# A two-layer kernel with routed experts: the block list in two parts, and results stored at the addresses of their rows

## The reference

```python
x = x + mix(_layernorm(x))              # layer 0: a token-wise mixing step
# layer 0: nine experts, every token goes to two of them
logits = xf @ Wr                        # xf = _layernorm(x), 4096 x 128; Wr 128 x 9
topk_w, topk_idx = top_k(softmax(logits), 2)
gate   = silu(einsum('th,ehi->tei', xf, Wg))        # Wg, Wu 9 x 128 x 352
hidden = gate * einsum('th,ehi->tei', xf, Wu)
out    = einsum('tei,eih,te->th', hidden, Wd, cw)   # Wd 9 x 352 x 128
x = x + out
x = x + attention(_layernorm(x))        # layer 1: 16 heads, causal
x = x + moe64(_layernorm(x))            # layer 1: 64 experts, top 8, and a shared one
```

## Time and profile before

| | |
|---|---|
| median of 3 runs | 1076.92 us (1076.34 to 1079.82) |
| the profiled execution | 1076.07 us, of which the span of the trace is 1074.3 us |
| PE busy | 930.9 us (87%) |
| DVE busy | 833.0 us (78%) |
| ACT busy | 700.1 us (65%) |
| POOL busy | 455.2 us (42%) |
| chain that ended last | PE 74%, POOL 7%, DVE 6%, issue 4%, ACT 4%, DMA 3% |
| routing and scatters | 0 to 136 us of the span |
| the 72 blocks | 136.5 to 295.5 us |

### The profile page before, as it was taken

How to read it: one execution, slowest core, us unless ns; L and a number is a source line. 1 busy time by engine, 2 the same in 40 slices (tenths; PEclk the granted TensorE clock), 3 DMA queues, 4 the chain that set the end, 5 groups by cost and what they waited for, 6 DMA issues and landing times.

```text
span 1074.3 us, 20489 instructions
## 1 busy us (share of the span) xinstructions
PE 930.9 (87%) x6052; PEld 744.9 (69%) x6052; DVE 833.0 (78%) x1945; ACT 700.1 (65%) x1390; POOL 455.2 (42%) x523
## 2 busy tenths in 40 slices
PE   3652089999828999999999998999999999999998
PEld 2541079999825677776776766777777777777786
DVE  6888267777649888888888767888887979787965
ACT  4751045555436787787787766777778777777876
POOL 1278750000066565565564422444434443443433
PEclk8655589999959999999999999999999999999999
DMA  8011112222121011011010003847566575748483
GB/s 258 23 49 57 56 53 67 65 63 64 55 59 28 21 31 31 21 31 31 21 31 21 11 2 88 177 110 165 135 140 147 129 162 114 169 106 189 98 195 77
DMA packets 63921, 89.99 MB, mean 84 GB/s; under 512 B 16559, under 2 KB 54610, under 8 KB 59730
## 3 DMA queue, kind: packets, MB, share of 16 engines
q1 hardware_dynamic: 59136, 80.33, 31.2%
q0 software_dynamic: 4096, 8.40, 2.7%
q10 hardware_dynamic: 594, 0.09, 0.0%
HBM read 70.90 MB, written 17.89 MB: 83 GB/s over the span
## 4 chain that ended last, share of the span: by engine, by line
PE 74%; POOL 7%; DVE 6%; issue 4%; ACT 4%; DMA 3%; SPq 1%; POOLq 0%; DVEq 0%; ACTq 0%
POOL xs L666 6%; PE ps L2216 6%; PE ps L2198 5%; PE ps L2200 5%; PE ps L2199 5%; PE ps L2218 5%; PE ps L2217 5%; PE ps L2002 3%; PE ps L1943 3%; PE ps L2065 3%; PE ps L2048 3%; PE ps L2020 2%; PE ps L1921 2%; PE ps L1922 2%; PE ps L1923 2%
## 5 line engine op out<-in xcount | busy, mean ns | idle before, releaser
L822 POOL TENSOR_TENSOR hl<-h,hh 128x512 fp32r<-128x512 f32 x128 | 167.8, 1311 | 256.3 <-ACT hh L1100 256.3
L1100 ACT ACTIVATE hh<-h 128x512 fp32r<-128x512 f32 (+1 forms) x264 | 165.2, 626 | 33.0 <-DVE h L1778 30.2
L1778 DVE TENSOR_TENSOR h<-ps,cwB 128x512 f32<-128x512 f32 x192 | 130.1, 683 | 45.3 <-ACT ps L1089 33.8
L1678 DVE TENSOR_REDUCE nm<-ps 128x4 f32<-128x512 f32 (+1 forms) x128 | 116.4, 952 | 35.1 <-PE ps L2048 33.1
L1089 ACT ACTIVATE ps<-ps 128x512 f32<-128x512 f32 x192 | 111.6, 581 | 36.3 <-PE ps L2200 35.2
L720 POOL DMA_INDIRECT yg<-ys,gps x64 | 62.5, 976 | 166.0 <-issue 154.6
L2198 PE MATMUL ps<-xh,wh 128*128 128x512 f32 x256 | 103.7, 405 | 0.1
L2216 PE MATMUL ps<-hh,wh 128*128 128x512 f32 x256 | 102.8, 402 | 0.6 <-POOL hl L822 0.6
L1785 DVE TENSOR_TENSOR hl<-h,hh 128x512 fp32r<-128x512 f32 (+1 forms) x136 | 95.7, 703 | 9.8 <-ACT hh L1100 8.6
L2200 PE MATMUL ps<-xh,wl 128*128 128x512 f32 x256 | 100.1, 391 | 0.0
L2218 PE MATMUL ps<-hh,wl 128*128 128x512 f32 x256 | 100.0, 391 | 0.0
(11 more groups left out here) (340 smaller groups left out, 2683.2 us busy)
## 6 DMA issues: line engine op xcount, KB each, us to landing
cwB<-cwd SPq DMA_DIRECT2D x32, 1536.0 KB, 14.8
cwd<-cwS SPq DMA_DIRECT2D x64, 96.0 KB
xb<-xs SPq DMA_DIRECT2D x72, 64.0 KB, 1.8
ys<-yb SPq DMA_DIRECT2D x72, 64.0 KB, 1.6
x_res<-in_L_attn_x_dram SPq DMA_DIRECT2D x4, 512.0 KB, 6.4
wst<-in_L_ffn_W_up_dram SPq DMA_DIRECT2D x32, 64.0 KB, 2.2
wst<-in_L_ffn_W_down_dram SPq DMA_DIRECT2D x32, 64.0 KB, 2.0
out_dram<-y SPq DMA_DIRECT2D x8, 256.0 KB, 13.4
```

Of the source, the lines that this page charges most:

```text
L822: pool.tensor_tensor(hl4[:, slot(u), :], h4[:, slot(u), :], hh4[:, slot(u), :].bitcast(F32), op=ALU.subtract).then_inc(u_hlp, 1)
L1100: act.activation(hh4[r, slot(u), :], h4[r, slot(u), :], ACT.Copy).then_inc(u_hh, 1)
L1678: ins = dve.tensor_reduce(nm[:, u, 4 * g:4 * g + 4], o, axis=AX.X, op=ALU.max, negate=True)
L1778: dve.tensor_tensor(h4[:, slot(u), :], first, second, op=ALU.mult).then_inc(u_h, 1)
```

## The change

The block list is made in two parts. The first, `blk_a`, holds NFULL = 24 blocks that rounds 0 and 1 fill completely whatever the routing is. It is worked out from the counts after round 1, in small steps between the routing steps of rounds 1 to 3, and is ready behind `sel` of round 3. SP waits for it, and only for the scatters of rounds 0 and 1, and starts loading blocks, while POOL still scatters rounds 2 and 3. The whole list, `blk_b`, is worked out in single steps of 1 or 2 small DVE operations at the first ten blocks (`whole_list_step`), with nine small matmuls on PE at block 10 (`listed`), and serves blocks 24 to 71.

A block's result is now stored in `ys` at the same rows as the block has in `xs`. So `gpi` is a plain cast of the rows, but each store reads its address with a register load too. `ys` has as many rows as `xs`, rounded up to 39936, and SP fills it with zeros at the start: 13 DMAs of 3 x 1024 rows of 512 bytes, 20.4 MB in all, before them one DMA of 0.5 MB for the spare rows of `xs`. SP waits for them after it has loaded the first four blocks. The nine zero-row DMAs behind the lists' ends now stand in SP's stream after its first four steps.

The low and high parts of weight pieces 6 to 8 (Wd) are made by POOL ahead of its first scatter; DVE makes pieces 2 to 5 in step 5, and nothing of the weights is left for the first block.

```diff
+            sp_.wait_ge(consts, 1)
+            sp_.dma_start(xs[0:SPARE, :].rearrange("(k p) d -> p k d", p=P),
+                          zrow[:, :].unsqueeze(1).broadcast_to([P, SPARE // P, P])).then_inc(tails_in, 16)
+            sp_.wait_ge(consts, 2)
+            for n in range(0, NFILL, 3):
+                sp_.dma_start(ys[n * FILL * P:(n + 3) * FILL * P, :].rearrange("(n p k) d -> p n (k d)", n=3, k=FILL),
+                              zfill[:, :].unsqueeze(1).broadcast_to([P, 3, FILL * D])).then_inc(tails_in, 16)
+
+            def rows_of(blocks, b):
+                return ds(sp_.value_load(blocks[0:1, ds(b, 1)], min_val=0, max_val=SPARE + E1 * REG - P), P)
+
+            def load_block(b, u, blocks):
+                sp_.dma_start(xb[:, u, :], xs[rows_of(blocks, b), :]).then_inc(xb_in[u], 16)
...
-            def store_block(b, u):
+            def store_block(b, u, blocks):
                 sp_.wait_ge(yb_r, b + 1)
-                sp_.dma_start(ys[ds(b * P, P), :], yb[:, u, :]).then_inc(ys_out[u], 16)
+                sp_.dma_start(ys[rows_of(blocks, b), :], yb[:, u, :]).then_inc(ys_out[u], 16)
+
+            def next_block(b, u, blocks):
+                sp_.wait_ge(xT_r, b + 1)
+                load_block(b + 4, u, blocks)
+                if not isinstance(b, int) or b >= 2:
+                    store_block(b - 2, (u - 2) % 4, blocks)
+
+            sp_.wait_ge(lists, 1)
+            for s in range(2):
+                sp_.wait_ge(scat[s], SCATTERED)
+            for b in range(4):
+                load_block(b, b, blk_a)
+            sp_.wait_ge(tails_in, 16 * (NFILL // 3 + 1))
+            for b in range(4):
+                next_block(b, b, blk_a)
             sp_.wait_ge(tails, 1)
             for e in range(E1):
...
+            with sp_.Fori(1, NFULL // 4 - 1) as it:
+                for u in range(4):
+                    next_block(it * 4 + u, u, blk_a)
+            sp_.wait_ge(lists, 2)
+            sp_.wait_ge(tails_in, 16 * (NFILL // 3 + 1 + E1))
             for s in range(2):
                 sp_.wait_ge(scat[s], SCATTERED * (NR // 2))
...
+            for u in range(4):
+                next_block(NFULL - 4 + u, u, blk_b)
...
+            with sp_.Fori(NFULL // 4, NBLK // 4 - 1) as it:
                 for u in range(4):
-                    b = it * 4 + u
-                    sp_.wait_ge(xT_r, b + 1)
-                    load_block(b + 4, u)
-                    store_block(b - 2, (u - 2) % 4)
+                    next_block(it * 4 + u, u, blk_b)
             for b in range(NBLK - 6, NBLK):
-                store_block(b, b % 4)
+                store_block(b, b % 4, blk_b)
...
+            for piece in range(6, 9):
+                src, hi, lo, arrived, n = weight_piece(piece)
...
+                own.link(pool.tensor_copy(hi, src))
+                own.link(pool.tensor_tensor(lo, src, hi.bitcast(F32), op=ALU.subtract))
+                pool.sem_inc(w_lo, 1)
             for r in range(NR):
                 scatter_round(r)
...
+            def first_matches():
+                own3.need(own3.n)
+                dve.tensor_tensor(onehot[lv, :, 0:NFULL], listed(NFULL), lq[lv, 6, :].unsqueeze(2).broadcast_to([LEV, E1, NFULL]),
+                                  op=ALU.is_equal).then_inc(sl2, 1)
+
+            def first_blocks():
+                dve.wait_ge(rk2, NR)
+                dve.tensor_copy(blk_a[0:HALF + 1, :], bank[1][0:HALF + 1, 0:NFULL]).then_inc(lists, 1)
...
+                        if r == 2:
+                            first_shares()
+                        if r == 3:
+                            first_blocks()
...
                 if k == NR + 1:
-                    for piece in range(2, 5):
+                    first_matches()
+                    dve.memset(hb[:, :, I1:IP], 0.0).then_inc(consts, 1)
+                    for piece in range(2, 6):
                         w_low(piece)
```

More of the change, by code:

```diff
@@ L630, in _ @@
             own.done(pool.memset(ones[:, :], 1.0))
-            for dst, pattern, cm, b0 in ((rev9[:, :, :], [[0, RT], [-1, E1]], 0, E1), (off9[:, :], [[REG, E1]], 0, 0),
-                                         (base[:, :], [[REG, E1]], 0, 0),
-                                         (prow[:, :], [[0, E1]], 1, 0), (iblk[:, :], [[1, NBLK]], 0, 0)):
+            own.done(pool.memset(lev_w[:, :, :], 0.0))
+            own.done(pool.memset(spare[:, :], 0.0))
+            own.done(pool.memset(lcnt[:, E1:E1 + 1], float(NFULL + 1)))
+            for dst, pattern, cm, b0 in ((rev9[:, :, :], [[0, RT], [-1, E1]], 0, E1), (half_off[:, :, :], [[0, 2], [-REG, E1]], 0, -SPARE),
+                                         (base[:, :], [[REG, E1]], 0, SPARE), (w99[:, :, :], [[1, E1], [-1, E1]], 0, 0),
+                                         (prow[:, :], [[0, E1]], 1, 0), (entry[:, :], [[1, NBLK]], 0, 1)):
                 own.done(pool.iota(dst, pattern=pattern, base=b0, channel_multiplier=cm,
@@ L1132, in _ @@
         def _(dve):
-            dve.memset(stv[R1:P, :, JC - 1, :], 0.0)
+            dve.memset(stv[R1:P, :, JC - 1, :], 0.0).then_inc(wd_in, 16)
             dve.wait_ge(x_in[0], 16)
@@ L1368, in _ @@
[L1368 to L1401, removed]
@@ L1429, in y_out @@
                 dve.wait_ge(y_r, b + 1)
+                if isinstance(b, int) and b == LISTED:
+                    dve.wait_ge(rk2, NR + 2)
+                    found, rows_ = bank[1][0:HALF + 1, 2 * D:2 * D + NBLK], slice(0, HALF + 1)
+                    own3.done(dve.scalar_tensor_tensor(onehot[rows_, 0, :], found, 0.0, spare[rows_, :], ALU.is_equal, ALU.mult))
+                    own3.need(own3.n)
+                    dve.tensor_tensor(blk_b[rows_, :], found, onehot[rows_, 0, :], op=ALU.add).then_inc(lists, 1)
                 if again is not None:
@@ L1433, in y_out @@
                                   axis=AX.X, op=ALU.add).then_inc(yb_r, 1)
[L1435 removed]
             x_lo(0, 0)
[L1437 to L1438 removed]
+            for b in range(4 * LEAD):
                 x_lo(b + 1, (b + 1) % 2)
[L1440 to L1441 removed]
                 h_of(b, b % 2)
[L1443 to L1444 removed]
                 if b >= 1:
@@ L1482, in _ @@
             dve.wait_ge(c_in, 16 * 7)
-            own = Tickets(dve, dve_c1)
+            own = Tickets(dve, dve_c1, own3.n)
             wqk = wqkv[:, 0:2 * D].rearrange("p (g s) -> p g s", s=S)
@@ L1845, in biases, with listed @@
                               skip_group_check=True)
+            def listed(n, o):
+                pe.wait_ge(sl2, NR + 2 * (n - 1))
+                for e in range(E1):
+                    ins = pe.matmul(o, lev_w[lv, e, :], onehot[lv, e, 0:o.shape[-1]], start=e == 0, stop=e == E1 - 1,
+                                    skip_group_check=True)
+                ins.then_inc(rk2, 1)
             def pe_round(k, one, mix, two):
```

213 lines of the change are left out of this document (147 added, 66 removed).

## The result

The changed kernel takes **1093.34 us** (median; 1088.75 to 1094.27, 4 runs) against 1076.97 of the kernel before (1076.34 to 1079.82, 4 runs): ratio 1.0138, 95% interval 1.0104 to 1.0173. The forecast was 1086, slower, with a range of 1075 to 1108. The profiled execution took 1094.27 us, the slowest of the four, with a span of 1092.5, 18.2 more than the span before.

A forecast was written before the change was run, and what follows sets the result against it. PE bounds the block stage before, SP after the change. SP's stream, +3.3, and long issues, +6.2, sum to +9.5: 1076.07 becomes 1085.6, with 0.85 to the median 1086 us; range 1075 to 1108.

The forecast's parts named there:

- long issues: SP's stream: DMA issues longer than usual, 3.9% of the time, no longer hidden by PE's pace; +6.2 us.
- The bound: Block loop: the store's register load adds 0.64 us, SP takes 2.51 a block over PE's 2.09; chance 0.70, 1078 to 1095.
- cheap register load: Rival at SP's turn: up to 0.22 us a store PE keeps the pace; 1052 us, chance 0.10.
- Zero rows: Nine DMAs, 10.1 us, ahead of block 8's load: PE idle 7 us, its clock may fall, costing nothing more.
- POOL is done at 42 and the first scatter at 44.0 isn't moved: Ahead of the scatters: POOL's three Wd weight pieces take 13.4 us and delay nothing.
- The list steps: DVE and POOL, routing: small operations for the first list add 2.4 us, so it is ready at 98.7.
- a first transpose after 105: Sign at the first block, expected near 101.4: later than 105 means the fill, the scatters or the list are wrong.
- The fill: SP's queue behind Wd: 21.0 MB at 294 GB/s, done at 99.5, delaying the first load by nothing; bounds 0 and +25.
- slow fill: Rival in SP's queue: below 294 GB/s block loads stand behind the fill; +25 at 219, 1111 us, chance 0.06.
- crowded-out scatters: Rival at rounds 0 and 1: the fill slows scatters; +10 (1096) at half speed, +30 (1116) if held up; chance 0.10.
- Low clock in the block stage: Rival: PE, busy five sixths of the time, runs a quarter of the blocks at low clock; +29, 1115 us, chance 0.04.
- the stream: SP's loads, stores and zero rows from 98.7 to the last store landing at 298.7, against 295.46 before; +3.3 us.

The follow-up runs named there:

- e7: The kernel before with one more register load ahead of each store, its value not used: 1108.86 us, ratio 1.0282.
- e4: The changed kernel with SP's loops written out, each block's address read once and kept in a register from load to store: 1063.98 us, ratio 0.9857.
- e5: e4 with the nine zero-row DMAs issued one a step behind steps 3 to 11, not all behind step 3: 1056.49 us, ratio 0.9789.
- e8: The kernel before with only POOL making the parts of weight pieces 6 to 8 ahead of its first scatter: 1086.94 us, ratio 1.0082.
- e2: The changed kernel with weight pieces 6 to 8 made by ScalarE and DVE again, none by POOL: 1086.06 us, ratio 1.0069.
- e6: The changed kernel with the edits of e4, e5 and e2 together: 1048.16 us, ratio 0.9733.
- e9: The kernel before with only the 13 fill DMAs into ys behind Wd in SP's queue, and one memset: 1078.17 us, ratio 1.0003.
- e1: The changed kernel with results stored at rows 128 b, so stores read no address (gathers then read other rows): 1066.74 us, ratio 0.9889.

## Why the prediction was right, and where its sizes were off

| step | predicted | measured |
|---|---|---|
| first list ready | 98.7 | 104.9 |
| first transpose | 101.4 | 107.9 |
| block 8 transposed | 127.5 | 134.6 |
| PE's wait there | 7 | 10.2 |
| turn of SP's loop | 10.04 | 10.03 to 10.31, last four turns |
| last transpose, long issues included | 294.0 | 299.1 |
| last store lands | 304.9 | 309.8 |
| span against before | +9.5 | +18.2 |

**The bound.** That the store's register load costs 0.64 us, makes SP's turn 10.04 us and puts SP ahead of PE as the bound, was right: from 198 on, the turns with no long issue in them take 10.03 or 10.04, and e7 and e4 show it from both sides: +31.3 when put in alone, -29.4 when taken out. The price came from comparing gaps in one turn of the earlier trace rows, load against store, not from the length of the read. The rival of a cheap register load is excluded.

**Zero rows.** Right in place and close in size: block 8 came 26.8 us behind the first transpose, where 26.1 were written (124.3 + 0.79 + 1.96 gives 127.1 and not 127.5, hence 25.7). PE's wait was put at 7 because it was taken to want block 8 "near 120"; eight blocks after the first it wanted it at 124.4 - 107.9 = 16.5 us, which would have been 117.9 in the prediction's times. The remark that the wait "costs nothing more, since SP sets the pace" fits the changed kernel, and so does "its clock may fall", with 0.50 from 134 to 137. Both lie on the path once the store's read is gone: e5 took 7.5 us off e4. What spreading would gain with the read still there wasn't tried.

**The mis-sized step: "POOL is done at 42 and the first scatter at 44.0 isn't moved".** POOL was done at 41.7. But the step priced only POOL's own time and asked only whether POOL's next work would be late. DVE's operations on SBUF beside it were taken at their old lengths, and they are what the first scatter waits for. This term is 8 us, put at 0; e8 measured it as +9.4, e2 as -7.3, e6 against e5 as -8.3. The list steps, put at 2.4, cost only about 0.5 (`sel` of the last round moved by 8.5 where that of the first had moved by 8.0), and so the first list came 6.2 late, not 8. The prediction's own sign misled too: a first transpose after 105 was to mean that the fill, the scatters or the list were wrong. It came at 107.9, and e8, e9 and e2 show that it was none of them.

**Long issues.** +6.2 was put in for them. From block 8 to the last transpose SP's stream took 164.5 us against 160.3 without long issues, 4.2 more, but only 1.6 of that are long issues: the timeline of SP has six above 0.45 us there, the longest 0.89, where the kernel before had ten in 132 us, 5.1 above the usual in all. Another 1.5 are three waits for `yb`, for which nothing was forecast, the longest 1.1 us at 155, right behind the list's matmuls on PE. So long issues did not come with SP's time as the share of 3.9% assumed.

**The fill.** Taken at 294 GB/s and done at 99.5; from 28 to 60 the queues moved 417 GB/s, nearly all of it the fill, and it was done by about 83. Cost 0 as forecast, and e9 excludes the rivals of a slow fill and of crowded-out scatters. Scatters beside it do land later, 6.8 us after their issue for 2.2, but that never reached what anyone waits for; whether it comes from the order of packets no run shows.

**Low clock in the block stage.** As the rival had it, a quarter of the blocks at the low clock, it is excluded: 0.99 in the window of 116 us. Ahead of that window it did fall, behind the wait for block 8 (0.50 from 134 to 137) and behind one of 3.5 us for block 12 (0.66 from 147 to 152); SP's pace hid most of it.

**What is left over.** 14.3 of the 18.2 us had come about by the last store. The other 3.9 lie behind it, where nothing was changed and nothing forecast. Two windows of the changed kernel at the start of the attention stage, then those at the same distance (within 1 us) behind the last store in the kernel before:

```profile
345.00:350.00 5.00, 2.91 (x15) 2.34 (x14) 4.66 (x8) 2.04 (x5) 4.12 (x7) 0.61 0.01 2
350.00:355.00 5.00, 5.00 (x24) 4.72 (x25) 4.21 (x8) 3.32 (x4) 3.74 (x4) 0.50 0.14 39
```

```profile
330.00:335.00 5.00, 2.67 (x16) 1.86 (x17) 4.90 (x9) 2.04 (x5) 4.76 (x8) 1.00 0.00 0
335.00:340.00 5.00, 4.55 (x34) 3.60 (x33) 4.59 (x12) 4.52 (x6) 3.28 (x5) 1.00 0.12 30
```

PE idles about as much in the first of each pair, yet the granted clock is 0.61 and 0.50 there, half speed at 1.2 GHz, where it had stayed at 1.00, and PE does 24 matmuls where it did 34. The third window, to 360, is at 0.87, so some 10 us were at half speed, which costs 5 where PE is the bound and less elsewhere; from the first matmul of L2126 (before: L2002) to the end of its last the attention stage took 326.4 us against 323.8, and 1.3 came behind it. The traces of e1, e2, e4 and e5 show the same extra stretch at the same distance, e6, e7 and e9 a shorter one, e8 none. These are single executions, e7, e8 and e9 are the kernel before with one thing added, and the kernel before itself ranges over 7 us in 15 runs (mean clock 0.933 in the one of 1076.23, 0.926 in the one of 1083.05). So the change needn't be what brings the stretch; why the clock fell in one and not in the other isn't settled.

So the forecast of 1086 was 7 us low. The missing term on POOL and DVE, 8 us, is about its size, and the 3.9 behind the last store are partly made up by the list steps and the stream, which came 1.9 and 2.0 us cheaper than forecast.

## What to carry to other kernels

Price every instruction that a change gives to a queue that issues DMAs, and compare that queue's turn with the turn of the engine it feeds: a sequencer appears in no busy table, and here one register load of 0.27 us, 0.64 with its surroundings, ate a gain of 30 us. An address that was read once can stay in a register, and fixed work of such a queue, 10 us in one piece here, did better as pieces of 1.1 us between the loads, which the blocks loaded ahead mostly cover. When work moves to another engine, look not only at when that engine is free but at what its neighbour does on the same memory meanwhile.

## What the runs showed of the hardware that was not expected

- A `value_load` whose result is not used costs the queue as much as one that is: 0.43 us a block over PE's pace (e7), against 0.41 in the changed kernel (29.4 us over 72 blocks, e4).
- Some of DVE's float32 operations wait for whole POOL operations on SBUF: eight TENSOR_SCALAR of 0.26 us took 8.64 in all beside POOL's casts and subtractions of 1.2 and 2.6 us, and operations with two inputs in SBUF were held up too (0.69 to 2.10 in e8), while those reading PSUM kept their 0.21 to 0.75 and a TENSOR_REDUCE with its one input in SBUF its 0.22. POOL's own operations were hardly longer for it (2.61 to 2.95).
- One core wrote from SBUF to HBM, nearly all in 4 KB pieces, at 417 GB/s (28 to 60), faster than the 394 to 401 of the best slices of the earlier trace rows.
- Small scatters beside such a stream land 4.6 us later (6.8 for 2.2, e9), at an unchanged rate of issue.
